# Loads split in place, a second buffer for the folded sequences, and a weight product in the butterfly stage of a post-LN decoder layer

## The chip, the cores and the metric

The kernel runs on one core of a Trainium2 chip. The time is device time in microseconds (us) from the start of the launch to its end. A core has a matrix engine (TensorE; PE in the profile, its weight loads PEld), three engines for elementwise work (VectorE or DVE, ScalarE or ACT, GpSimd or POOL), and SyncE (SP), which here only starts transfers. The on-chip memory has 128 partitions; a tile is partitions x elements. TensorE's results go to a memory of their own (PSUM), in which this kernel's products are 128 x 512 tiles.

## What is computed

A decoder layer on x of shape (4, 1024, 512) in float32, with a context of shape (4, 2048, 384): windowed self-attention, then a cross-attention block, then a feed-forward block whose hidden layer passes two butterfly transforms. What the change touches is this part of the reference:

```python
V = x_vision @ Wv                                   # (., 2048, 384) @ (384, 512)
c_t = einsum('btg,bgd->btd', attn_mean, V)
x = layernorm(x_text, g_norm_in, b_norm_in)
scale_in, shift_in = split(c_t @ W_film_in + b_film_in, 2)    # W_film: (512, 1024)
x = x * (1 + mod_gate * scale_in) + mod_gate * shift_in
Kf = rfft(K, n=2 * L); xf = rfft(x, n=2 * L, axis=1)
y = irfft(xf * Kf.T[None], n=2 * L, axis=1)[:, :L] + x * D_skip
scale_out, shift_out = split(c_t @ W_film_out + b_film_out, 2)
...
h = butterfly(x @ W_exp + b_exp, up_weights)        # 11 stages of 2x2 blocks on 2048 columns
h = butterfly(gelu(h + up_bias), down_weights)
y = h @ W_con + b_con + down_bias
```

## The kernel before

`decoder_layer` (L2985) runs nine stages one behind another: `taps` (L86), `butterfly` (L481), attention, keys, cross-attention, `film` (L1720, the conditioning), `dft` (L2023, the spectrum), `idft` (L2228, the inverse) and the feed-forward parts. A stage allocates its own on-chip tiles, ends at a barrier, and then GpSimd clears its semaphores one by one (L66). Within a stage the order on each engine is written out by hand, with semaphores between engines. A product in full float32 precision is `mm3` (L78): each operand is split into a high half (rounded to fp32r, by a ScalarE copy) and a low half (the difference, by a VectorE subtraction), and three products are added.

**Butterfly.** The stage multiplies the butterflies into the weights beforehand. Each matrix (`wc` = W_con for the down weights, `wT` = W_exp turned for the up weights) takes its four outer butterfly levels as passes over 8 block pairs of 128 rows. For each pair ScalarE scales two partners (`partners`, L647 and L648); for each group of two pairs VectorE makes four sums (`group`, L729 and L734). Four slots of partners lie between them, so ScalarE is at most two groups ahead. The seven inner levels are multiplied out by VectorE into 16 blocks (`low_blocks`, `e_up` and `e_dn`); TensorE multiplies these into `wT` (L597) and, after turning them (L605), into `wc` (L614). The order is: passes 0 to 3 of the first matrix (`wc`), with the copies of the turned W_exp in pass 1 (L673) and of the 16 products in passes 2 and 3; then passes 0 to 3 of the second (`wT`), in whose passes 1 and 2 ScalarE copies the turned down blocks (L655) and the 16 down products; then SyncE stores these (`w4`), and the final rows are turned (L624) and stored (`w3`). ScalarE's and VectorE's first work waits for `s_wc` and `s_cols`, all of W_con and all ten small loads of columns and biases on SyncE's queue.

**Conditioning.** TensorE turns Wv (L1836) and makes 12 blocks Wv times W_film (4 quarters `f` by 3 row blocks `c`, L1848), each of four 128x512 products. ScalarE writes a block's high half times the gate (L1891), VectorE its low half. `wfilm` holds one film matrix, so W_film_out is loaded when six blocks are done. TensorE waits for all 12, then 32 tiles follow, with 4 x 3 x 3 = 36 products each.

**Spectrum.** Four DFT matrices of 128x2048 are loaded by SyncE into the two halves of `raw` in turn, and split (L2144, L2172). Then the taps are loaded into `raw`, TensorE reverses the second half of the rows (L2106), VectorE folds (sum and difference, L2179 and L2180, into `uvf`), and both are split into `uv` (L2150, L2186). Five sequences, taps first and then four of the batch, each have 8 chunks of 24 products. For the taps VectorE makes `kc` and `ks` (L2197 to L2202) from each chunk, for the others four products with them (L2218); GpSimd adds these (L2092, L2093) and ScalarE's queue stores. The fold of the next sequence stands ahead of chunk 6, but `uv` is single: its high halves wait for the last product of the sequence before (L2149), and `split` is the first thing of the next one.

**Inverse.** Four matrices go through the two halves of `mraw`, then eight spectrum chunks through the two of `raw`. The products wait for all four matrices and then for each chunk. Each sequence has four row tiles; TensorE ends one with 8 x 2 x 3 products, and ScalarE copies one half of the result (L2355). The next sequence's chunks are split after the last products that read the old ones (`s_used`), two at a time as `raw` allows.

## Time and profile before

| | us |
|---|---|
| median of 3 runs | 4975.23 (4973.64 to 4977.94) |
| profiled execution | 4974.19 |
| its span, first to last instruction | 4972.5 |
| butterfly stage, from its first transfer | 272.84 |
| conditioning stage | 2468.49 |
| spectrum stage | 2835.96 |
| inverse stage | 3161.19 |

| engine | busy us | share of the span |
|---|---|---|
| TensorE (PE) | 4046.5 | 81% |
| VectorE (DVE) | 2692.0 | 54% |
| ScalarE (ACT) | 1435.4 | 29% |
| GpSimd (POOL) | 1301.9 | 26% |

TensorE is busy for most of the span, but the shares are means over nine stages with different limits. A stage's cost is what stands between its first transfer and the barrier behind it, so the four edited stages are read by their timelines: one line is a run of like instructions of an engine, with its start, its busy time, and in brackets how long the engine had been idle and what released it. In windows each engine has its busy time and count, then come the granted clock as a share of TensorE's full speed (1.00 is 2.4 GHz, 0.50 is 1.2 GHz), the mean share of the transfer engines and the traffic.

### The profile page before, as it was taken

The page shows a single profiled execution, that of the slowest core. Times are in us where ns is not written, and L with a number is a line of the kernel's source. Part 1 is how long each engine was busy: PE and PEld are TensorE (multiplying, and loading weights), DVE is VectorE, ACT ScalarE, POOL GpSimd, SP SyncE. Part 2 cuts the span into 40 slices and gives each one's busy share as a digit, 9 for nine tenths or more (in the row PEclk, how much of TensorE's full clock was granted, in tenths as well). Part 3 has the DMA queues.
Part 4 walks back from the last instruction along what each step waited for, and adds up shares of the span by engine and source line. Part 5 has one row for each costly group of instructions (what it writes and reads, how often), then busy time and mean ns, then how long its engine had stood idle before and what let it go on. Part 6 is the DMA issues. An engine that isn't in the chain of part 4 may idle for free. (4 is left out here: it accounts for less than half of the span.)

```text
span 4972.5 us, 63780 instructions
## 1 busy us (share of the span) xinstructions
PE 4046.5 (81%) x20652; PEld 3295.3 (66%) x20652; DVE 2692.0 (54%) x9090; ACT 1435.4 (29%) x2190; POOL 1301.9 (26%) x1123
## 2 busy tenths in 40 slices
PE   6833898756878866678689788695999999999998
PEld 4712777636767765667658666574888787887886
DVE  8644545438988989989535445322443445322222
ACT  2344333235555544455310000121211112111111
POOL 0000000002121120121136414102576775433332
PEclk8666999878888887788899889897999999999999
DMA  1134222260110100100124422334122223100000
GB/s 56 37 117 119 68 83 79 66 193 28 30 42 12 44 26 10 39 30 12 41 92 140 140 73 110 120 127 139 50 71 65 74 74 99 33 26 20 22 25 20
DMA packets 244966, 329.93 MB, mean 66 GB/s; under 512 B 67013, under 2 KB 125253, under 8 KB 242375
## 3 DMA queue, kind: packets, MB, share of 16 engines
q1 hardware_dynamic: 152568, 175.70, 11.9%
q10 hardware_dynamic: 89568, 142.64, 8.5%
q0 software_dynamic: 2560, 8.39, 0.4%
q8 instruction: 121, 1.98, 0.2%
q14 instruction: 149, 1.21, 0.1%
HBM read 217.55 MB, written 109.10 MB: 66 GB/s over the span
## 5 line engine op out<-in xcount | busy, mean ns | idle before, releaser
L1496 PE MATMUL xa_ps_t<-xa_diag,xa_s_buf 128*128 128x128 f32 x4096 | 503.0, 283 | 161.7 <-DVE xa_s_buf L1677 96.8
L1496 PEld LDWEIGHTS xa_ps_t<-xa_diag,xa_s_buf 128*128 128x128 f32 x4096 | 486.9, 198 | 192.0 <-DVE xa_s_buf L1677 114.3
L1625 DVE MAX8 xa_cand<-xa_s_buf 128x8 f32<-128x64 f32 x4096 | 534.9, 217 | 115.6 <-issue 56.9
L2938 DVE CAST m_act_hl<-m_g 128x512 fp32r<-128x512 f32 x256 | 137.7, 538 | 831.9 <-ACT m_g L2806 831.9
L2632 POOL TENSOR_TENSOR m_act_hl<-m_g,m_act_hl 128x512 fp32r<-128x512 f32 x256 | 355.5, 1389 | 660.0 <-DVE m_act_hl L2938 660.0
L2806 ACT ACTIVATE m_g<-m_ps_h,m_b 128x512 f32<-128x512 f32 x256 | 176.1, 688 | 1096.2 <-PE m_ps_h L82 1091.1
L1441 POOL TENSOR_TENSOR xa_aT<-xa_a,xa_aT 128x512 fp32r<-128x512 f32 x128 | 159.7, 1269 | 1006.6 <-ACT xa_a L1561 1006.6
L80 PE MATMUL m_ps_h<-m_hT,m_w 128*128 128x512 f32 x1024 | 413.7, 404 | 6.4 <-issue 4.3
L80 PE MATMUL m_ps_o<-m_w,m_act_hl 128*128 128x512 f32 x1024 | 406.9, 397 | 0.7 <-POOL m_act_hl L2632 0.7
L82 PE MATMUL m_ps_o<-m_w,m_act_hl 128*128 128x512 f32 x1024 | 406.6, 397 | 0.0
L81 PE MATMUL m_ps_o<-m_w,m_act_hl 128*128 128x512 f32 x1024 | 406.5, 397 | 0.0
L82 PE MATMUL m_ps_h<-m_hT,m_w 128*128 128x512 f32 x1024 | 406.2, 397 | 0.0
L81 PE MATMUL m_ps_h<-m_hT,m_w 128*128 128x512 f32 x1024 | 406.0, 396 | 0.0
L1540 ACT ACTIVATE xa_s_buf<-xa_ps_s 128x2048 f32<-128x2048 f32 x128 | 239.7, 1873 | 403.1 <-PE xa_ps_s L1477 328.6
L1677 DVE SCALAR_TENSOR_TENSOR xa_s_buf<-xa_s_buf,xa_top,xa_prob 128x2048 f32<-128x2048 f32 x128 | 294.7, 2344 | 4.4 <-ACT xa_prob L1551 0.8
L1477 PE MATMUL xa_ps_s<-xa_ks,xa_qs 128*128 128x512 f32 x512 | 189.0, 501 | 105.7 <-ACT xa_s_buf L1540 83.9
L1551 ACT ACTIVATE xa_prob<-xa_s_buf,xa_nmax 128x2048 f32<-128x2048 f32 x128 | 252.4, 2000 | 31.7 <-DVE xa_s_buf L1677 31.7
L80 PE MATMUL xa_ps_ac<-xa_ctx_hl,xa_aT 128*128 128x384 f32 x512 | 206.5, 403 | 50.9 <-POOL xa_aT L1441 50.9
L80 PEld LDWEIGHTS m_ps_h<-m_hT,m_w 128*128 128x128 f32 x1024 | 193.4, 189 | 56.1 <-issue 11.4
L80 PEld LDWEIGHTS m_ps_o<-m_w,m_act_hl 128*128 128x128 f32 x1024 | 193.1, 189 | 48.8 <-POOL m_act_hl L2632 2.0
L82 PEld LDWEIGHTS m_ps_o<-m_w,m_act_hl 128*128 128x128 f32 x1024 | 193.6, 189 | 47.0
L81 PEld LDWEIGHTS m_ps_o<-m_w,m_act_hl 128*128 128x128 f32 x1024 | 193.4, 189 | 47.1
(366 smaller groups left out, 8119.5 us busy)
## 6 DMA issues: line engine op xcount, KB each, us to landing
at_xk<-in_x_dram SPq DMA_DIRECT2D x128, 128.0 KB, 2.7
spectrum<-df_yo ACTq DMA_DIRECT2D x32, 512.0 KB, 2.8
id_raw<-spectrum SPq DMA_DIRECT2D x32, 512.0 KB, 3.8
m_xt<-x ACTq DMA_DIRECT2D x64, 256.0 KB, 3.5
ky_raw<-in_ctx_dram SPq DMA_DIRECT2D x16, 768.0 KB, 6.3
xa_ks<-kt SPq DMA_DIRECT2D x48, 256.0 KB
...
```

The costliest lines, as they stand in the source:

```text
L80: pe.matmul(out, w_hi, m_lo, start=start, stop=False)
L81: pe.matmul(out, w_lo, m_hi, start=False, stop=False)
L82: return pe.matmul(out, w_hi, m_hi, start=False, stop=stop)
L1441: pool.tensor_tensor(aT[:, 1, 4 * g:4 * g + 4, :], a32[:, g % 2, :, :], aT[:, 0, 4 * g:4 * g + 4, :].bitcast(F32), ALU.subtract).then_inc( ...
L1477: last = pe.matmul(ps_s[:, c, :], qs[:, t % 2, h, :], ks[:, h, c * 512:(c + 1) * 512], start=True, stop=True)
L1496: last = pe.matmul(ps_t[:, c // 4, c % 4, :], s_buf[:, t % 2, h, k0:k0 + P], diag[:, h, :], start=(h == 0 and c % 4 == 0), stop=(h == HEAD ...
L1540: act.activation(s_buf[:, t % 2, h, :], ps_s[:, :, :].rearrange("p c n -> p (c n)"), ACT.Copy).then_inc(s_sc, 1)
L1551: act.activation(prob[:, h % 2, :], s_buf[:, t % 2, h, :], ACT.Exp, bias=nmax[:, t % 2, h:h + 1], scale=SCALE).then_inc(s_exp, 1)
L1625: dve.max(out=ranks[h][:, :, g], in_=s_buf[:, t % 2, h, g * SEG:(g + 1) * SEG])
L1677: dve.scalar_tensor_tensor(out=s_buf[:, t % 2, h, :], in0=s_buf[:, t % 2, h, :], scalar=top[:, t % 2, h, TOPK - 1:TOPK], in1=prob[:, h % 2 ...
L2632: pool.tensor_tensor(lo, g32[:, :], hi.bitcast(F32), ALU.subtract).then_inc(s_gl, 1)
L2806: act.activation(g32[:, :], ps_h[:, n % 2, :], ACT.Gelu, bias=b1[:, cur, n:n + 1]).then_inc(s_g, 1)
```

## The change

The diff has four parts, here by stage and with what falls away mostly left out, as it stands in the code above.

**Butterfly.** The order of the loads is new: the down columns first, W_con in four pairs of pieces with a semaphore each, then b_exp, the up columns and the rest; ScalarE starts its loads behind its first pair. The stage also makes the 12 blocks Wv times W_film. Each film matrix is loaded into the memory of `low_up` or `low_dn` once the inner levels of that matrix are multiplied out. TensorE makes six blocks behind the 16 up products, two behind down product 7 and four behind down product 15; VectorE copies the turned Wv between groups of pass 1, and the blocks (times the gate, into `fo`, two slots) between groups of passes 0, 1 and 3 of the second matrix; SyncE stores them to `wf` in DRAM, six ahead of the down rows and six behind.

```diff
+        for k in range(TOP):
+            sp.dma_start(col_dn[:, k, :, :], A["L0_ffn_down_weights"][LOW + k].rearrange("(q p) i j -> p q (i j)", p=P)).then_inc(s_cdn, 16)
...
+            for h in (2 * k, HC // 2 + 2 * k):
+                sp.dma_start(wc[:, h:h + 2, :], A["L0_ffn_W_con"][h * P:(h + 2) * P, :].rearrange("(c p) n -> p c n", p=P))\
+                  .then_inc(s_wc[k], 16)
...
+        for k in range(TOP):
+            sp.dma_start(col_up[:, k, :, :], A["L0_ffn_up_weights"][LOW + k].rearrange("(q p) i j -> p q (i j)", p=P)).then_inc(s_cup, 16)
+        sp.dma_start(low_dn[:, 0:LEN], A["butterfly_down"]).then_inc(s_ld, 16)
...
+        sp.wait_ge(s_wx[1], 16)
+        sp.dma_start(wv[:, :, :], A["L0_xattn_Wv"].rearrange("(c p) n -> p c n", p=P)).then_inc(s_wv, 16)
...
+        for k, (done, name) in enumerate(((s_eu, "in"), (s_ed, "out"))):
+            sp.wait_ge(done, 1)
+            sp.dma_start(films[k], A[f"L0_xattn_W_film_{name}"].rearrange("(c p) n -> p c n", p=P)).then_inc(s_film[k], 16)
+        def film_stored(n):
+            sp.wait_ge(s_fc, n + 1)
+            sp.dma_start(wf_out[n % VC, :, n // VC, :], fo[:, n % 2, :]).then_inc(s_fs[n % 2], 16)
+        for n in range(FILM):
+            film_stored(n)
         for n in range(HC):
             sp.wait_ge(s_dc, n + 1)
             sp.dma_start(w4_out[n * P:(n + 1) * P, :], out_t[:, n % 4, :]).then_inc(s_out[n % 4], 16)
+        for n in range(FILM, 2 * FILM):
+            film_stored(n)
...
+        def film(n):
+            k, q, c = n // FILM, n % FILM // VC, n % VC
+            if n % FILM == 0:
+                pe.wait_ge(s_film[k], 16)
+                pe.wait_ge(s_wvc, VC)
+            if n >= 2:
+                pe.wait_ge(s_fc, n - 1)
+            for e in range(DC):
+                last = pe.matmul(ps_w[:, n % 2, :], wvT[:, e, c * P:(c + 1) * P], films[k][:, e, q * D:(q + 1) * D],
+                                 start=(e == 0), stop=(e == DC - 1))
+            last.then_inc(s_fp, 1)
...
-        pe.wait_ge(s_cols, 16 * 10)
+        pe.wait_ge(s_cup, 16 * 5)
         pe.wait_ge(s_eu, 1)
...
+        for n in range(FILM):
+            film(n)
...
+            if h == HC // 2 - 1:
+                film(FILM)
+                film(FILM + 1)
+        for n in range(FILM + 2, 2 * FILM):
+            film(n)
...
+        act.wait_ge(s_cdn, 16 * 4)
         for q in range(HC // 2):
+            if q % 2 == 0:
+                act.wait_ge(s_wc[q // 2], 32)
             partners(0, 0, q)
+            if q == 0:
+                act.dma_start(low_up[:, 0:LEN], A["butterfly_up"]).then_inc(s_lu, 16)
+                w_exp(0)
+                w_exp(1)
+        act.wait_ge(s_cup, 16 * 5)
...
+        def film_copied(n):
+            dve.wait_ge(s_fp, n + 1)
+            if n >= 2:
+                dve.wait_ge(s_fs[n % 2], 16 * (n // 2))
+            dve.tensor_scalar(fo[:, n % 2, :], ps_w[:, n % 2, :], gate[:, 0:1], None, ALU.mult).then_inc(s_fc, 1)
+        dve.wait_ge(s_cdn, 16 * 4)
         for g in range(GROUPS):
+            dve.wait_ge(s_wc[g], 32)
             group(0, 0, g)
...
+                if i == 1 and g < VC:
+                    dve.wait_ge(s_wvt, g + 1)
+                    dve.tensor_copy(wvT[:, :, g * P:(g + 1) * P], ps_w[:, g % 2, :].rearrange("p (e q) -> p e q", e=DC))\
+                       .then_inc(s_wvc, 1)
...
+                if i == 0:
+                    film_copied(g)
+                if i == 1 and GROUPS + g < FILM:
+                    film_copied(GROUPS + g)
+                if i == TOP - 1:
+                    film_copied(FILM + g)
+        for n in range(FILM + GROUPS, 2 * FILM):
+            film_copied(n)
```

```diff
+    wf = scratch("wf", [VC, P, 4, D])
+    stage_butterfly(nc, A, w3, b3, w4, wf)
...
+    stage_film(nc, A, wf, x1, ac, xin, so, sh)
```

**Conditioning.** The products are gone. Four chunks of 768 KB come from `wf` into `raw`, which is the memory of the low half of the tile `wf`; ScalarE writes the high halves, VectorE the low ones in place, and the first tile's products wait for one chunk at a time.

```diff
+wf = sb("wf", [P, 2, NF, VC, D], F32R)
+raw = nc.alloc_sbuf_tensor_at("fi_raw", [P, NF, VC, D], F32, offset=at + 4 * NF * VC * D)
...
+            sp.dma_start(raw[:, f, :, :], wf_in[:, :, f, :].rearrange("c p n -> p c n")).then_inc(s_wf[f], 16)
...
+                if first:
+                    pe.wait_ge(s_fol, f + 1)
+                else:
                     pe.wait_ge(s_fr, NF * (t - 1) + f + 1)
...
+        def weights_hi(f):
+            act.wait_ge(s_wf[f], 16)
+            act.activation(wf[:, 0, f, :, :], raw[:, f, :, :], ACT.Copy).then_inc(s_foh, 1)
...
+        def weights_lo(f):
+            dve.wait_ge(s_foh, f + 1)
+            dve.tensor_tensor(wf[:, 1, f, :, :], raw[:, f, :, :], wf[:, 0, f, :, :].bitcast(F32), ALU.subtract).then_inc(s_fol, 1)
...
+        dve.wait_ge(s_ld, 16 * 5)
+        dve.tensor_scalar(bf[:, :, :], bf[:, :, :], gate[:, 0:1], None, ALU.mult)
...
         norm(0, 0)
+        for f in range(NF):
+            weights_lo(f)
+        dve.drain()
         tiles(dve, tile)
```

**Spectrum.** All four matrices are loaded at once, each into the memory of its own low half (`mraw`), two by SyncE behind the taps and two by ScalarE. The fold is done in place in `x`. `uv` has two buffers. The high halves of a sequence wait for the sequence before the last; for the batch the fold stands ahead of chunk 5 and the split ahead of chunk 7, for the first of them (`split(1)`) behind the taps' last chunk. The loops are written out.

```diff
+mraw = nc.alloc_sbuf_tensor_at("df_mraw", [P, 2, 2, TC, 512], F32, offset=at + 4 * 2 * 2 * TC * 512)
...
+x = sb("x", [P, 2, TC, D])
+uv = sb("uv", [P, 2, 2, 2, TC, D], F32R)
...
+        def load(src, first, n):
+            if n:
+                sp.wait_ge(s_lo, 2 * n)
...
+            sp.dma_start(x[:, 0, :, :], rows(src, first, S // 2).rearrange("(q p) d -> p q d", p=P)).then_inc(s_x, 16)
+        load(taps, 0, 0)
+        for n in (1, 3):
+            sp.dma_start(mraw[:, n // 2, n % 2, :, :], A["dft"][n // 2, n % 2].rearrange("(q p) m -> p q m", p=P)).then_inc(s_m[n], 16)
+        for b in range(B):
+            load(xin, b * S, b + 1)
...
                 if q == 0:
                     pe.wait_ge(s_lo, 2 * n + 1 + src)
+                if n == 0 and mq == 0:
+                    pe.wait_ge(s_ml, 2 * par + sd + 1)
...
+        for n in (0, 2):
+            act.dma_start(mraw[:, n // 2, n % 2, :, :], A["dft"][n // 2, n % 2].rearrange("(q p) m -> p q m", p=P)).then_inc(s_m[n], 16)
+        act.dma_start(tw[:, :, :], A["twiddle"].rearrange("i (q p) -> p i q", p=P), allow_slow_non_contiguous=True).then_inc(s_tw, 16)
...
         def hi(n):
             act.wait_ge(s_uv, n + 1)
-            act.wait_ge(s_f, MC * n)
+            if n >= 2:
+                act.wait_ge(s_f, MC * (n - 1))
             for i in range(2):
-                act.activation(uv[:, i, 0, :, :], uvf[:, i, :, :], ACT.Copy).then_inc(s_hi, 1)
...
+        matrix_hi(0)
+        hi(0)
+        for n in range(1, 4):
+            matrix_hi(n)
+        hi(1)
...
+                if q == MC - 2 and b + 2 <= B:
...
+            dve.tensor_tensor(x[:, 1, :, :], x[:, 0, :, :], ps_rev[:, :, :], ALU.subtract)
+            dve.drain()
+            dve.tensor_tensor(x[:, 0, :, :], x[:, 0, :, :], ps_rev[:, :, :], ALU.add)
...
         fold(0)
+        matrix_lo(0)
         split(0)
+        for n in range(1, 4):
+            matrix_lo(n)
...
+            if q == MC - 1:
+                split(1)
+        for b in range(B):
             for q in range(MC):
-                k = q % 2
...
+                if q == MC - 3 and b + 2 <= B:
                     fold(b + 2)
...
+                if q == MC - 1 and b + 2 <= B:
+                    split(b + 2)
```

**Inverse.** All matrices and all chunks are loaded at once, in place as well; a chunk has its own place and semaphore, and is reloaded when its last product of the sequence before is done.

```diff
+y = sb("y", [P, 2, MC, 2, D], F32R)
+mraw = nc.alloc_sbuf_tensor_at("id_mraw", [P, 2, 2, TC, 512], F32, offset=at + 4 * 2 * 2 * TC * 512)
+raw = nc.alloc_sbuf_tensor_at("id_raw", [P, MC, 2, D], F32, offset=at + 4 * 2 * 2 * 2 * TC * 512 + 4 * MC * 2 * D)
...
+        def chunk(b, q):
+            if b:
+                sp.wait_ge(s_used, MC * (b - 1) + q + 1)
+            sp.dma_start(raw[:, q, :, :], y_in[b:b + 1, q].rearrange("o i p d -> p (o i) d")).then_inc(s_y[q], 16)
...
+        chunk(0, 0)
+        matrix(1)
+        chunk(0, 1)
+        matrix(3)
+        for q in range(2, MC):
+            chunk(0, q)
+        for b in range(1, B):
             for q in range(MC):
...
+                chunk(b, q)
...
+                        if first and t == 0 and mq == 0:
+                            pe.wait_ge(s_ml, 2 * par + pm + 1)
...
+        for n in (0, 2):
...
-        hi(0)
+        hi(0, 0)
+        for n in range(2):
+            matrix_hi(n)
+        for q in range(1, 4):
+            hi(0, q)
+        for n in range(2, 4):
+            matrix_hi(n)
+        for q in range(4, MC):
+            hi(0, q)
```

Two engines' rows show what stands where. First TensorE in the butterfly stage, from the last up products to the turning of the down blocks (`bf_e_dn`), before:

```order
L596 MATMUL bf_ps_b<-bf_wT,bf_e_up 128x1 [waits bf_block_product_copied]
L597 MATMUL bf_ps<-bf_wT,bf_e_up 128x512
L605 MATMUL bf_ps_e<-bf_ident,bf_e_dn 128x128 [waits bf_groups_done,bf_down_blocks,bf_block_product_copied]
L605 MATMUL bf_ps_e<-bf_ident,bf_e_dn 128x128
L614 MATMUL bf_ps<-bf_wc,bf_eT 128x512 [waits bf_down_matrix_transposed_copied]
L605 MATMUL bf_ps_e<-bf_ident,bf_e_dn 128x128 [waits bf_down_matrix_transposed_copied]
```

and now (the left-out rows are three more blocks like the last shown; L666 was L605 and L675 was L614):

```order
L656 MATMUL bf_ps<-bf_wT,bf_e_up 128x512
L644 MATMUL bf_ps_w<-bf_low_up,bf_wvT 128x512 [waits bf_value_weights_turned_copied,bf_film_loaded0]
L644 MATMUL bf_ps_w<-bf_low_up,bf_wvT 128x512 x7
L644 MATMUL bf_ps_w<-bf_low_up,bf_wvT 128x512 [waits bf_film_product_copied]
L644 MATMUL bf_ps_w<-bf_low_up,bf_wvT 128x512 x3
...
L666 MATMUL bf_ps_e<-bf_ident,bf_e_dn 128x128 [waits bf_groups_done,bf_down_blocks,bf_block_product_copied]
L666 MATMUL bf_ps_e<-bf_ident,bf_e_dn 128x128
L675 MATMUL bf_ps<-bf_wc,bf_eT 128x512 [waits bf_down_matrix_transposed_copied]
```

Six blocks have moved between the up products and the down blocks; those from the third on wait for VectorE's copy.

VectorE in the spectrum stage at a change of sequence: the products of the last chunk and what follows, before:

```order
L2218 TENSOR_TENSOR df_prod<-df_ps,df_kc 128x512
L2218 TENSOR_TENSOR df_prod<-df_ps,df_ks 128x512
L2218 TENSOR_TENSOR df_prod<-df_ps,df_kc 128x512
L2218 TENSOR_TENSOR df_prod<-df_ps,df_ks 128x512
L2222 REGISTER_ALU
L2222 COMPARE_AND_BRANCH
L2186 TENSOR_TENSOR df_uv<-df_uvf,df_uv 128x2048 x2
L2218 TENSOR_TENSOR df_prod<-df_ps,df_kc 128x512
```

and now, from the fold ahead of chunk 5 (the L2269 rows are the products that were L2218, four to a chunk):

```order
L2226 TENSOR_TENSOR df_x<-df_x,df_ps_rev 128x2048
L2228 TENSOR_TENSOR df_x<-df_x,df_ps_rev 128x2048
L2269 TENSOR_TENSOR df_prod<-df_ps,df_kc 128x512
L2269 TENSOR_TENSOR df_prod<-df_ps,df_ks 128x512
L2269 TENSOR_TENSOR df_prod<-df_ps,df_kc 128x512
L2269 TENSOR_TENSOR df_prod<-df_ps,df_ks 128x512
L2269 TENSOR_TENSOR df_prod<-df_ps,df_kc 128x512
L2269 TENSOR_TENSOR df_prod<-df_ps,df_ks 128x512
L2269 TENSOR_TENSOR df_prod<-df_ps,df_kc 128x512
L2269 TENSOR_TENSOR df_prod<-df_ps,df_ks 128x512
L2234 TENSOR_TENSOR df_uv<-df_x,df_uv 128x2048 x2
L2269 TENSOR_TENSOR df_prod<-df_ps,df_kc 128x512
```

The two splits have moved from behind the sequence's last chunk to ahead of it, and the fold to two chunks ahead of them.

## Rows read from the trace of the kernel before

**Rows 1.** Timeline of the conditioning stage's start (columns as its first line), then windows, TensorE

```profile
start us, us, engine line op out<-in xcount [idle before <-releaser]
2468.49 0.34 SPq L1789 DMA_DIRECT2D fi_gate<-in_L_xattn_mod_gate_dram  x1
2483.85 1.28 DVE L1938 TENSOR_SCALAR fi_bf<-fi_bf,fi_gate 128x2048 f32<-128x2048 f32 x1 [48.97 <-DMA fi_bf<-_L_xattn_b_film_out_dram]
2485.22 0.76 DVE L1941 TENSOR_SCALAR fi_bf<-fi_bf 128x512 f32<-128x512 f32 x2
2487.54 22.95 PE L1848 MATMUL fi_ps_w<-fi_wfilm,fi_wvT 128*128 128x512 f32 x48 [0.69 <-ACT fi_wvT L1885]
2518.46 22.85 PE L1848 MATMUL fi_ps_w<-fi_wfilm,fi_wvT 128*128 128x512 f32 x48 [7.97 <-DMA fi_wfilm<-_L_xattn_W_film_out_dram]
2548.35 0.80 PE L80 MATMUL fi_ps_f<-fi_wf,fi_aT 128*128 128x512 f32 x1
...
core 0: us, PE busy (x), PEclk, DMA share, GB/s
2487.50:2493.30 5.80, 5.76 (x9) 0.63 0.00 0
2552.50:2560.00 7.50, 7.50 (x34) 0.95 0.01 3
```

**Rows 2.** Timeline of the spectrum stage from its start to its first product

```profile
2835.96 0.38 SPq L2066 DMA_DIRECT2D df_tw<-in_twiddle_dram  x1
2844.91 2.29 DVE L2172 TENSOR_TENSOR df_mats<-df_raw,df_mats 128x2048 fp32r<-128x2048 f32 x1 [14.70 <-ACT df_mats L2144]
2867.94 1.19 PE L2106 MATMUL df_ps_rev<-df_raw,df_flip 128*128 128x512 f32 x1 [38.52 <-DMA df_raw<-taps]
2883.59 0.79 PE L80 MATMUL df_ps<-df_uv,df_mats 128*128 128x512 f32 x1 [8.94 <-DVE df_uv L2186]
```

**Rows 3.** Timeline of spectrum stage at two changes of sequence, and a chunk's window

```profile
2932.84 0.75 DVE L2197 TENSOR_SCALAR df_prod<-df_ps,df_tw 128x512 f32<-128x512 f32 x1 [0.26 <-PE df_ps L82]
2946.11 0.69 DVE L2218 TENSOR_TENSOR df_prod<-df_ps,df_kc 128x512 f32<-128x512 f32 x1 [5.56 <-PE df_ps L82]
2990.91 2.89 DVE L2186 TENSOR_TENSOR df_uv<-df_uvf,df_uv 128x2048 fp32r<-128x2048 f32 x1 [0.73 <-issue]
2991.61 3.33 POOL L2093 TENSOR_TENSOR df_yo<-df_prod 128x512 f32<-128x512 f32 x1
...
core 0: us, PE busy (x) PEld busy (x) DVE busy (x) ACT busy (x) POOL busy (x), PEclk, DMA share, GB/s
...
3118.56:3124.00 5.44, 5.44 (x25) 4.50 (x24) 2.48 (x4) 0.00 (x0) 2.53 (x2) 1.00 0.26 96
```

**Rows 4.** Timeline of the inverse stage: first product, and row tiles' ends on ScalarE

```profile
3184.29 0.77 PE L80 MATMUL id_ps<-id_y,id_mats 128*128 128x512 f32 x1 [33.12 <-DVE id_y L2373]
3206.56 0.60 ACT L2355 ACTIVATE id_a_sb<-id_ps 128x512 f32<-128x512 f32 x1 [3.02 <-PEq L2320]
3229.92 0.60 ACT L2355 ACTIVATE id_a_sb<-id_ps 128x512 f32<-128x512 f32 x1 [10.33 <-PEq L2320]
3257.60 0.60 ACT L2355 ACTIVATE id_a_sb<-id_ps 128x512 f32<-128x512 f32 x1 [2.16 <-PEq L2320]
3269.78 0.60 ACT L2355 ACTIVATE id_a_sb<-id_ps 128x512 f32<-128x512 f32 x1 [10.24 <-PEq L2320]
```

**Rows 5.** Timeline of the butterfly stage's start: first transfer, ScalarE's first work

```profile
272.84 0.39 SPq L550 DMA_DIRECT2D bf_wc<-in_L_ffn_W_con_dram  x1
310.47 0.72 ACT L647 ACTIVATE bf_part<-bf_wc,bf_col_dn 128x512 f32<-128x512 f32 x1 [41.48 <-DMA bf_upb<-in_L_ffn_up_bias_dram]
321.66 0.58 ACT L673 ACTIVATE bf_wT<-bf_ps 128x512 f32<-128x512 f32 x1
```

**Rows 6.** Windows of the butterfly stage (columns as in Rows 3), and one timeline row

```profile
316.22:319.25 3.03, 0.00 (x0) 0.00 (x0) 2.83 (x5) 2.56 (x5) 0.00 (x0) 0.50 0.00 0
411.22:413.08 1.86, 1.22 (x4) 0.44 (x3) 1.03 (x3) 1.86 (x6) 0.00 (x0) 1.00 0.41 149
...
392.97 1.22 PE L614 MATMUL bf_ps<-bf_wc,bf_eT 128*128 128x512 f32 x1 [12.83 <-ACT bf_eT L655]
```

**Rows 7.** Windows of transfers: both queues (Rows 3's columns), then SyncE's alone

```profile
281.00:289.00 8.00, 1.91 (x8) 1.51 (x8) 0.00 (x0) 0.00 (x0) 0.00 (x0) 0.50 1.00 418
...
core 0: us, , PEclk, DMA share, GB/s
2863.00:2864.00 1.00, 0.50 1.04 406
```

314 lines of the change are left out of this document (119 added, 195 removed).

## Prediction

> **What bounds the kernel now.** The stages stand one behind another, each ended by a barrier, so each is read by itself. I read the timeline by engine from a stage's first transfer to its first product, then the places where TensorE stops in the steady part, and the windows for clock and traffic. Outside four stages nothing is edited.
>
> The conditioning stage has its first transfer at 2468.49 and its first tile product at 2548.35: 79.9 us in which TensorE makes 12 folded blocks, six behind each 2 MB load [rows 1]. A block is 48/6 = 8 records, 3.43 us at full clock; VectorE's share of it never waits on anything but this product. The stage behind that is TensorE's.
>
> The spectrum stage goes from 2835.96 to 2883.59 (47.6 us) without a product [rows 2]: four matrices through two buffers, then the taps, then reverse, fold and split in a row. Afterwards TensorE runs a chunk in 5.44 us (distance of two of VectorE's product groups, 3118.56 to 3124.00) and stops at each change of sequence: 2932.84 to 2946.11 is 13.27 instead of 5.44 [rows 3].
>
> The inverse stage starts its products at 3184.29, 23.1 us in; its first row tile ends 22.3 us later, where a later one takes 12.2 (3257.60 to 3269.78); a change of sequence makes two tiles last 27.7, 28.1 and 28.3 (the first is in [rows 4]) instead of 24.4.
>
> The butterfly stage is bound by ScalarE and VectorE in turns. Nothing is computed from 272.84 to 310.47, since ScalarE waits for the last of eleven loads [rows 5]. Then VectorE needs 3.03 us per group of block pairs (316.22 to 319.25), and in the two middle passes of the second matrix ScalarE needs 1.86 per pair (411.22 to 413.08) [rows 6].
>
> **Transfers.** One queue alone moves 406 GB/s, two queues together 418 [rows 7]. So I divide all bytes on both queues by 400 GB/s and let two queues share evenly. The Trainium skill (DMA: Bandwidth & Descriptors, section "Issuing engines are not separate DMA queues") says that starting transfers from two engines saves only the issue. The rows agree; were the queues additive instead, the taps would land 5 us earlier.
>
> **Conditioning stage: minus 56.4.** Transposes, 24 + 24 products and the 12 evictions go. Left ahead of the first tile are the loads. They ended at 2483.85 with 4.25 MB on one queue; now it is 5.4 MB with the tile loads, 1.15 MB or 2.9 us more: 2486.7. Then the bias scaling (1.28 + 2 x 0.76 with its drains, 2.9), the normalisation of 512 columns (0.57) and the low half of the first block, 1536 columns (1.72), both at 2.29 us per 2048 [rows 2]: product at 2491.9. 2548.35 - 2491.9 = 56.4; the other three low halves (5.2) lie beside the first tile's 10.7 us of products. Bounds: loads at 2484 or 2490, 53 to 59.
>
> **Spectrum stage, start: minus 18.** Six MB go at once. The taps (2 MB, SyncE's queue) come in while ScalarE's queue moves two matrices: 4 MB, 10.5 us, behind 1.9 of start and with 1.2 to the reversal as before: 2849.5 instead of 2867.94. The chain from there took 15.65 us; it gets 0.4 longer, as the first matrix's low half (2.29) now stands between fold and split and only 1.9 of it lies beside ScalarE's copy. If the taps' queue is served first, 23; if served last, 13.
>
> **Spectrum stage, changes of sequence: minus 19.** The excess over 5.44 is 7.8 (2932.84 to 2946.11), 8.2, 9.5 and 8.6, by the same reading. The second buffer lets ScalarE's and VectorE's split run ahead, but the split of the first sequence is written behind VectorE's last tap chunk, so it starts at the time it has now: no gain there. For the other three, VectorE folds before chunk 5 and splits before chunk 7. ScalarE's copies end 5.4 us after chunk 6's products, VectorE's first half then lands 0.4 us past the end of chunk 7, and its last products 1.1 past. That is 1.1 us with nothing in the way. Against it stands that the split now meets GpSimd's sums: where they met, VectorE's half took 2.89 instead of 2.29 and GpSimd's op 3.33 instead of 1.3 [rows 3]. That adds up to 2. I take 2.3 each: 26.3 - 6.9 = 19 (16 to 23).
>
> **Inverse stage: minus 21.5.** 8 MB start at once. By the same rate matrix 0 lands at 3169.5, its halves are done at 3173.8, and the product starts some 10.5 us earlier. Matrix 3 is complete at 3187.6 and the eight chunks' low halves follow every 1.2 us to 3192.5, so the first tile ends near 3195.5 instead of 3206.56: 11 (7 if TensorE is at its low level there). At a change of sequence a chunk is reloaded when its last product is done: 1.3 us of transfer, 3.6 to land, 2.3 to split, needed 12.2 after. It fits with 4 us to spare, so 3.3 + 3.7 + 3.9 = 10.9 goes; I take 10.5.
>
> **Butterfly stage: plus 11.** Here work is added to the engines that bound it.
> 1. The columns come first and the big weight in four parts, so pass one starts near 281.5 and ends near 297, 28 us earlier. But ScalarE's copies of the turned up-weight wait for the up-columns, which stand behind the 4 MB and share with ScalarE's own 4 MB: about 301 instead of 321.66 [rows 5]. Lead 20.7.
> 2. VectorE copies the turned value weights between its groups of pass two, and TensorE turns these behind all 16 up-weight groups. VectorE waits, and ScalarE's next pairs wait for VectorE: the lead falls to 15.
> 3. In the second matrix's first pass stand four gated copies (about 0.7 us each, by L2197's 0.75 in [rows 3]). TensorE makes blocks 2 to 5 in it, each waiting for the copy two before; the last ends near 388. Only then does it turn the down blocks, and ScalarE waits for those (TensorE waits 12.8 us for its copy ahead of 392.97 now [rows 6]; it would be 380): lead 4.
> 4. SyncE stores block 5 ahead of the first down rows, so ScalarE's fifth eviction finds its buffer unstored: 4.2. Lead 0.
> 5. Blocks 6 and 7 stand between down products 7 and 8: 6.9 us less 2 of slack: lead -5.
> 6. Blocks 8 to 11 are tied to the last pass's groups; the last ends 6 us behind VectorE's last group, and the final transposes wait for it: lead -11.
> So the stage ends 11 us later. Bounds: -3 (loads 4 us earlier, half of 3 to 5 absent) to +25 (the blocks at TensorE's low level, 6.9 instead of 3.43 us, as the 0.63 clock at 2487.5 shows for the first [rows 1]). Fourteen more semaphores to clear, ten in the other stages: 1 us.
>
> **Sum.** 56.4 + 18 + 19 + 21.5 - 11 - 1 = 102.9. The profiled execution took 4974.19 us, 1.04 under the median: 4871.
>
> **Rivals.**
> - *The fold really hides.* If steps 3 to 5 cost nothing, the stage ends 15 - 6 = 9 us earlier instead of 11 later: 4851, and 4845 with the taps served first. For it: TensorE is idle for 12.8 us ahead of 392.97. Against: each wait named above stands ahead of the next in its engine's own order.
> - *Low clock for the blocks.* They come in spells with idle time between: +14 at half of them, 4885; +27 at all, 4898.
> - *VectorE and GpSimd block each other.* Both halves and both sums of a change alternate, and the split ends as late as now: up to 19 back, 4890. The Trainium skill (SBUF - State Buffer, section "SBUF: two separate sides") has a VectorE op with two SBUF inputs and a GpSimd op exclude each other for a whole instruction. By that rule GpSimd's 1.3 plus the rest of a 2.25 half is 3.3, which the trace agrees with.
> - *Slower than before.* TensorE enters the conditioning tiles without 46 us of products ahead. If it then stayed at its low level in them, a tile's 36 products would take 15.4 instead of 8.4 us: 7 us per tile, 32 tiles, 5095. It turns slower from the 15th such tile on. Against it: from 2552.5 the clock is 0.95 after 4 us of unbroken products [rows 1].
> - *Not what it says:* the first change of sequence, counted above.
>
> **How the numbers follow.** Forecast 0.66 (4858 to 4884), hidden fold 0.12, low clock 0.11, mutual blocking 0.09, slower 0.02. The range 4846 to 4896 leaves out the slow case, half of the hidden fold's tail and the full low clock. 0.2% is 10 us, about what a measurement can tell; all cases but the last lie over 70 us below: faster 0.97, same 0.01, slower 0.02.
>
> **What would show it.** First tile product 23 to 24 us behind the conditioning stage's first transfer; first spectrum product 29 to 30 us in; three of four changes of sequence under 3.5 us of excess, the first still near 8; inverse changes near zero; in the butterfly stage first work about 9 us in, SyncE's first down-row store late, and a stage end some 11 us later. I am wrong if products at a stage's start wait for another load, or if the butterfly's end comes earlier.

## Result and the profile after

The changed kernel takes 4882.44 us (median of 4 runs, 4880.04 to 4883.11) against 4975.86 (4973.64 to 4977.94): 0.9813 of the time before, with a 95% interval of 0.9801 to 0.9825. The forecast was 4871 with a range of 4846 to 4896: the direction and the range hold, and 11 us of the gain are missing.

The profiled execution took 4882.0 us with a span of 4880.3, against 4972.5 of span before. The page's first lines, engines (busy us, share of the span):

```profile
span 4880.3 us, 63397 instructions
...
PE 4037.1 (83%) x20652; PEld 3291.2 (67%) x20652; DVE 2698.5 (55%) x9097; ACT 1431.6 (29%) x2179; POOL 1299.0 (27%) x1123
```

TensorE does as many products as before (20652). Its busy time has fallen by 9.4 us (4046.5 to 4037.1); the rest of the gain, 82.8 us, is idle time. Where it went is read from the stages' starts. GpSimd clears a tile at the start of each stage, in the timeline (start, busy us, engine, line, tile, idle before and its releaser):

```profile
272.54 0.20 POOL L608 MEMSET bf_ident<- 128x128 f32 x1 [11.07 <-POOLq L66]
485.70 0.20 POOL L985 MEMSET at_ident<- 128x128 f32 x1 [212.46 <-POOLq L66]
2489.03 0.20 POOL L1884 MEMSET fi_ident<- 128x128 f32 x1 [15.39 <-POOLq L66]
2798.04 0.20 POOL L2073 MEMSET df_flip<- 128x128 f32 x1 [7.15 <-POOLq L66]
3091.68 0.20 POOL L2073 MEMSET id_flip<- 128x128 f32 x1 [4.96 <-POOLq L66]
3321.61 0.20 POOL L2653 MEMSET m_ident<- 128x128 f32 x1 [6.94 <-POOLq L66]
```

Differences of neighbouring starts give the stages; of the kernel before they come from the same rows of its trace.

| stage | before, us | after, us | difference | forecast |
|---|---|---|---|---|
| butterfly | 196.6 | 213.2 | +16.6 | +11 |
| conditioning | 367.5 | 309.0 | -58.5 | -56.4 |
| spectrum | 325.2 | 293.6 | -31.6 | -37 |
| inverse | 249.9 | 229.9 | -20.0 | -21.5 |
| all that is not edited | 3833.3 | 3834.6 | +1.3 | 0 |
| clearing of the new semaphores | | in the stages | | +1 |

The +1.3 of the last row but one is mostly spread. Over all twelve profiled kernels, this one and the one before among them, the cross-attention took 1400.5 to 1407.2 us and the attention 511.3 to 514.6. The stage of the keys is less clear: 84.5 us in the kernel before and 86.1 to 88.1 in all eleven others. With one profile of the kernel before, the runs don't show whether the change has a part in that. Each run also repeats stages whose code is the same as in another: in five profiles the changed butterfly stage took 211.5 to 213.2 us. So a difference of under 2 us between two stages says little.

**Conditioning.** The biases' load ends the wait 18.2 us into the stage, and the first tile product comes 22.6 us in (79.9 before, at 2548.35 in [rows 1]). Timeline, then windows (us, PE busy and count, granted clock, DMA share, GB/s):

```profile
2507.26 1.29 DVE L2040 TENSOR_SCALAR fi_bf<-fi_bf,fi_gate 128x2048 f32<-128x2048 f32 x1 [7.88 <-DMA fi_bf<-_L_xattn_b_film_out_dram]
2511.66 0.77 PE L80 MATMUL fi_ps_f<-fi_wf,fi_aT 128*128 128x512 f32 x1 [10.92 <-DVE fi_wf L1998]
...
2511.00:2513.00 2.00, 1.34 (x3) 0.50 0.00 0
2513.00:2515.00 2.00, 2.00 (x6) 0.50 0.00 0
2515.00:2520.00 5.00, 5.00 (x22) 0.97 0.00 0
```

The granted clock is 0.50, the lower level of 1.2 GHz, until 2515 and 0.97 behind it, after 3.3 us of unbroken products. So the tiles don't stay at the low level for want of the fold ahead of them.

**Spectrum.** The reversal starts 13.9 us in and the first product 28.9 us in [rows 2: 32.0 and 47.6]. Then a change of sequence as before (the taps' last chunk to the first of the next sequence), and a later one, from chunk 6's products over the split to the next sequence's first:

```profile
2811.94 1.19 PE L2155 MATMUL df_ps_rev<-df_x,df_flip 128*128 128x512 f32 x1 [20.45 <-DMA df_x<-taps]
2826.91 0.80 PE L80 MATMUL df_ps<-df_uv,df_mats 128*128 128x512 f32 x1 [9.44 <-DVE df_uv L2234]
...
2876.96 0.75 DVE L2248 TENSOR_SCALAR df_prod<-df_ps,df_tw 128x512 f32<-128x512 f32 x1
2890.47 0.69 DVE L2269 TENSOR_TENSOR df_prod<-df_ps,df_kc 128x512 f32<-128x512 f32 x1 [6.00 <-PE df_ps L82]
...
2926.58 0.69 DVE L2269 TENSOR_TENSOR df_prod<-df_ps,df_kc 128x512 f32<-128x512 f32 x1 [0.78 <-PE df_ps L82]
2931.05 2.92 DVE L2234 TENSOR_TENSOR df_uv<-df_x,df_uv 128x2048 fp32r<-128x2048 f32 x1 [1.99 <-ACT df_uv L2198]
2941.50 0.69 DVE L2269 TENSOR_TENSOR df_prod<-df_ps,df_kc 128x512 f32<-128x512 f32 x1 [2.93 <-PE df_ps L82]
```

The first change takes 13.51 for one chunk, 8.07 over the 5.44 of [rows 3]. The later one takes 14.92 for two chunks, 4.04 over 10.88; the other two read the same way give 4.02 and 3.98. VectorE waits 1.99 us for ScalarE's half ahead of the split. That was not in my sum.

**Inverse.** First product 12.8 us in, first row tile's end 35.4 us in [rows 4: 23.1 and 45.4]; the two tiles at a change take 24.4 (3150.43 to 3174.81), twice a single one:

```profile
3104.46 0.76 PE L80 MATMUL id_ps<-id_y,id_mats 128*128 128x512 f32 x1 [22.93 <-DVE id_mats L2432]
3127.06 0.60 ACT L2412 ACTIVATE id_a_sb<-id_ps 128x512 f32<-128x512 f32 x1 [7.35 <-PEq L2377]
3150.43 0.60 ACT L2412 ACTIVATE id_a_sb<-id_ps 128x512 f32<-128x512 f32 x1 [10.33 <-PEq L2377]
3174.81 0.60 ACT L2412 ACTIVATE id_a_sb<-id_ps 128x512 f32<-128x512 f32 x1 [4.14 <-PEq L2377]
```

**Butterfly.** Rows of the timeline of ScalarE, VectorE and SyncE, in order of time:

```profile
281.06 0.72 ACT L713 ACTIVATE bf_part<-bf_wc,bf_col_dn 128x512 f32<-128x512 f32 x1 [12.35 <-DMA bf_wc<-in_L_ffn_W_con_dram]
322.64 0.69 DVE L825 COPY bf_wvT<-bf_ps_w 128x512 f32<-128x512 f32 x1 [8.65 <-PE bf_ps_w L632]
390.06 0.28 ACT L721 ACTIVATE bf_eT<-bf_ps_e 128x128 f32<-128x128 f32 x1 [8.82 <-PE bf_ps_e L666]
...
401.21 0.32 SPq L588 DMA_DIRECT2D wf<-bf_fo  x1
401.58 0.43 SPq L594 DMA_DIRECT2D w<-bf_out_t  x1
404.12 0.60 ACT L727 ACTIVATE bf_out_t<-bf_ps 128x512 f32<-128x512 f32 x1 [4.96 <-DMA w<-bf_out_t]
416.19 0.28 ACT L721 ACTIVATE bf_eT<-bf_ps_e 128x128 f32<-128x128 f32 x1 [5.85 <-PE bf_ps_e L666]
...
451.09 0.75 DVE L811 TENSOR_SCALAR bf_fo<-bf_ps_w,bf_gate 128x512 f32<-128x512 f32 x1 [2.25 <-PE bf_ps_w L644]
454.52 0.75 DVE L811 TENSOR_SCALAR bf_fo<-bf_ps_w,bf_gate 128x512 f32<-128x512 f32 x1 [2.68 <-PE bf_ps_w L644]
```

ScalarE starts 8.5 us in instead of 37.6 [rows 5], and then five waits follow: VectorE 8.65 us for TensorE to turn Wv, ScalarE 8.82 for the down blocks turned behind block 5, 4.96 for a down row's store that stands behind block 5's on SyncE's queue, 5.85 behind blocks 6 and 7, and at the end VectorE for the last two blocks. These two are 3.43 us apart: a block at full clock. Not all blocks ran so. TensorE's rows, then windows (us, PE busy and count, granted clock, DMA share, GB/s):

```profile
373.32 16.59 PE L644 MATMUL bf_ps_w<-bf_low_up,bf_wvT 128*128 128x512 f32 x32 [10.60 <-DVE bf_fo L811]
437.62 16.87 PE L644 MATMUL bf_ps_w<-bf_low_dn,bf_wvT 128*128 128x512 f32 x32 [8.72 <-DVE bf_fo L811]
...
373.30:379.60 6.30, 6.28 (x9) 0.58 0.23 88
437.60:444.20 6.60, 6.58 (x9) 0.56 0.21 79
444.20:454.50 10.30, 10.30 (x26) 1.00 0.20 76
```

These are blocks 2 to 5 and blocks 8 to 11. TensorE had been idle for 10.60 and 8.72 us ahead of them, and the first block of each run took 6.3 and 6.6 us at a granted clock of 0.58 and 0.56. Four blocks at full clock are 13.7 us, so the two runs are 2.9 and 3.2 us longer. The first ends where the down blocks are turned, for which ScalarE waits 8.82; the second ends in VectorE's last copy.

### The profile page after: what moved, and what is told of

It is laid out like the page before. It is cut to its first block and busy times, and to the rows that moved or that the text cites. A ratio compares the mean times of both kernels' runs of the same rounds, so it can differ in the third digit from the quotient of the medians.

```text
span 4880.3 us, 63397 instructions
## 1 busy us (share of the span) xinstructions
PE 4037.1 (83%) x20652; PEld 3291.2 (67%) x20652; DVE 2698.5 (55%) x9097; ACT 1431.6 (29%) x2179; POOL 1299.0 (27%) x1123
## 3 DMA queue, kind: packets, MB, share of 16 engines
q1 hardware_dynamic: 151976, 177.79, 12.2%
## 5 line engine op out<-in xcount | busy, mean ns | idle before, releaser
L80 PE MATMUL xa_ps_ac<-xa_ctx_hl,xa_aT 128*128 128x384 f32 x512 | 206.7, 404 | 48.1 <-POOL xa_aT L1530 48.1
L80 PEld LDWEIGHTS m_ps_h<-m_hT,m_w 128*128 128x128 f32 x1024 | 193.3, 189 | 55.9 <-issue 11.3
L80 PEld LDWEIGHTS m_ps_o<-m_w,m_act_hl 128*128 128x128 f32 x1024 | 193.2, 189 | 48.6 <-POOL m_act_hl L2705 2.0
L82 PEld LDWEIGHTS m_ps_o<-m_w,m_act_hl 128*128 128x128 f32 x1024 | 193.5, 189 | 46.9
L82 PEld LDWEIGHTS m_ps_h<-m_hT,m_w 128*128 128x128 f32 x1024 | 193.5, 189 | 46.9
```

The lines of the kernel that those rows point to most:

```text
L80: pe.matmul(out, w_hi, m_lo, start=start, stop=False)
L82: return pe.matmul(out, w_hi, m_hi, start=False, stop=stop)
```

## Experiments

Of the kernels below all but the last two were run once; they are compared by the stages of their profiles. The lead used below is worked out from VectorE's timeline: the start of its n-th group of block pairs, counted from the stage's start, in the kernel before less that in the kernel at hand.

### The new order of loads alone

The kernel before with only this part of the diff, no block in the stage:

```diff
-sp.dma_start(wc[:, :, :], A["L0_ffn_W_con"]...).then_inc(s_wc, 16)
+for k in range(TOP):
+    sp.dma_start(col_dn[:, k, :, :], ...).then_inc(s_cdn, 16)
+for k in range(4):
+    for h in (2 * k, HC // 2 + 2 * k):
+        sp.dma_start(wc[:, h:h + 2, :], ...).then_inc(s_wc[k], 16)
```

> The kernel before with the new order of loads of the butterfly stage alone: no products of Wv and W_film in it, the conditioning, spectrum and inverse stages as before. In the changed kernel VectorE's groups stand 20.0 us earlier in the stage at the end of pass one than before, and the stage ends 16.6 us later. If the new order of loads is worth that lead and everything given back comes from the 12 blocks, the stage takes 196.6 - 18 = about 178 us (some 2 us less than the 20, as W_exp's first rows are asked for 8 us later), and the run about 4957 us. Rival: the lead cannot be kept in any case, because the copies of the turned W_exp in pass 1 wait for rows of W_exp that are asked for later and share the engines with W_con; then the stage takes 188 to 197 us and the run 4967 to 4975.

Measured: stage 177.4 us, run 4958.6. The lead is 28.9 us at the first group, 20.9 at the end of pass 0 (ScalarE waits 4.8 us each for W_con's third and fourth pair of pieces, which are under way together with W_exp), and 19.2 to 19.4 from the second group of pass 2 to the last. So this order is worth 19.2 us for good, and the 12 blocks, their loads, copies and stores cost 213.2 - 177.4 = 35.8 us where they stand.

### One store moved

```diff
-for n in range(FILM):
+for n in range(4):
     film_stored(n)
 for n in range(HC):
+    if n in (2, 4):
+        film_stored(3 + n // 2)
     sp.wait_ge(s_dc, n + 1)
```

> The changed kernel with one thing moved: SyncE stores blocks 4 and 5 behind down rows 1 and 3 instead of ahead of down row 0. In the changed kernel ScalarE waits 4.96 us for a down row's store in the middle of the second matrix's pass 1. If this wait is on the path, as my step 4 has it, the butterfly stage takes 213.2 - 5 = 208 us and the run 4877. Rival: ScalarE's wait only covers one that is there anyway, the next one (for the down blocks turned behind blocks 6 and 7) grows by what is saved, and the stage stays within 1 us of 213.

Measured: stage 206.7 us, 6.5 less; run 4879.63. The wait was on the path. The table below shows it between groups 21 and 22. The 1.5 us beyond the 4.96 are within what the same stage varies by.

### The blocks spread over the stage

The pieces on TensorE; copies and stores follow them.

```diff
     pe.matmul(ps[:, h % 2, :], blk, wT[:, h, 0:D], start=True, stop=True).then_inc(s_mm, 1)
-for n in range(FILM):
-    film(n)
+    if h >= HC // 2:
+        film_part((h - HC // 2) // DC, h % DC)
+film(2)
...
 down_turned(0)
+down_turned(1)
+film(3)
+film(4)
+film(5)
...
-    if h == HC // 2 - 1:
-        film(FILM)
-        film(FILM + 1)
-for n in range(FILM + 2, 2 * FILM):
+    film_part(FILM + h // DC, h % DC)
+for n in range(FILM + 4, 2 * FILM):
     film(n)
```

> The changed kernel with the 12 blocks at other places of the butterfly stage, the same instructions otherwise: the turned Wv copied in pass 2 instead of 1 of the first matrix; blocks 0 and 1 one product at a time behind up products 8 to 15, block 2 behind those; both first down blocks turned ahead of blocks 3 to 5; blocks 6 to 9 one product at a time behind the 16 down products; only blocks 10 and 11 behind them; copies and stores to match. If the cost of the blocks is that others wait for TensorE in order, and not their work, the lead of some 20 us is mostly kept: stage 213 - 28 = 185 us (180 to 192), run about 4854. Rival: TensorE itself is the bound in the second matrix (its low clock makes a block 6.9 us), then the stage takes over 200 us.

Measured: stage 191.9 us, 21.3 less than in the changed kernel; run 4861.07. The blocks now cost 14.5 us. I expected 185, so 7 us of the gain are missing, but the rival's 200 did not come. The products are the same in both; it is who waits behind them that changed. The rest of the loss was read from this trace. VectorE waits for the store of block 0, which SyncE holds behind the load of W_film_out, and ScalarE for VectorE in turn:

```profile
372.55 0.75 DVE L825 TENSOR_SCALAR bf_fo<-bf_ps_w,bf_gate 128x512 f32<-128x512 f32 x1 [3.35 <-DMA wf<-bf_fo]
376.25 0.72 ACT L727 ACTIVATE bf_part<-bf_wT,bf_col_up 128x513 f32<-128x513 f32 x1 [4.36 <-DVEq L819]
```

### ScalarE's copies

```diff
+def film_scaled(n):
+    act.wait_ge(s_fp, n + 1)
+    act.wait_ge(s_fs[n % 2], 16 * (n // 2))
+    act.wait_ge(s_fc, n)
+    act.activation(fo[:, n % 2, :], ps_w[:, n % 2, :], ACT.Copy, scale=gate[:, 0:1]).then_inc(s_fc, 1)
...
         partners(1, i, q)
+        if i == 0 and q % 2:
+            film_scaled(2 + q // 2)
+        if i == TOP - 1 and q in (1, 4, 7):
+            film_scaled(FILM + 3 + q // 3)
...
+sp.wait_ge(s_wx[1], 32)
 for k, (done, name) in enumerate(((s_eu, "in"), (s_ed, "out"))):
...
+    if k == 0:
+        film_stored(0)
```

> The kernel with the blocks spread over the butterfly stage (191.9 us), with the waits that its trace shows taken away: the store of block 0 ahead of the load of W_film_out on SyncE (VectorE waited 3.35 us for it), W_film_in loaded behind the last rows of W_exp (2.3 us lost in pass 1), the stores of blocks 6 to 8 behind two more down rows (1.33 and 1.18 us), and the copies in the passes that VectorE bounds (0 and 3, seven of 0.7 us) made by ScalarE. If each of these is on the path by itself, the stage takes 191.9 - 3.4 - 2.3 - 2.5 - 4.9 = 179 us, within 2 us of the stage without any block (177.4). Rival: ScalarE at 2.46 of 3.03 us per group has no room for a copy of 0.6 and its waits, and the stage stays over 185 us.

Measured: stage 185.9 us, run 4856.47. I expected 179. The copies in passes 0 and 3 are free on ScalarE (the lead stays at 11.2 to 11.6 through pass 3, where VectorE's copies took 0.7 each); the wait for block 0's store is gone, but another of the same length stands in its place, ahead of the copy of block 3. ScalarE's row, SyncE's two, the time from the second of these to its landing, and a window of TensorE:

```profile
372.16 0.69 ACT L749 ACTIVATE bf_fo<-bf_ps_w,bf_gate 128x512 f32<-128x512 f32 x1 [3.35 <-issue]
...
362.26 0.37 SPq L589 DMA_DIRECT2D bf_low_dn<-_L_xattn_W_film_out_dram  x1
363.10 0.34 SPq L584 DMA_DIRECT2D wf<-bf_fo  x1
...
DMA to landing us min/median/max: 9.0/9.0/9.0
...
362.90:369.20 6.30, 6.17 (x10) 0.61 0.91 282
```

The timeline calls the releaser "issue", that is, it shows none. In its order ScalarE waits there for block 3 and for the store of block 1, whose slot the copy takes. Block 3's eight products (with two turned down blocks the ten of the window) had ended by 369.2, at a granted clock of 0.61. The store of block 1 started at 363.10, just behind the 2 MB load of W_film_out, and took 9.0 us to land, where a store of a block takes 2.3 in the median: 372.1. So it is again a store behind that load on SyncE, now block 1's, and the lead falls from 16.7 to 13.2.

The lead in us, by group (0 to 15 are the first matrix, 16 to 31 the second, four to a pass):

| group | loads alone | changed kernel | store moved | spread | ScalarE's copies |
|---|---|---|---|---|---|
| 3, end of pass 0 | 20.9 | 20.0 | 18.4 | 19.4 | 19.7 |
| 5, after the first copy of Wv | 20.9 | 10.9 | 9.6 | 19.4 | 19.7 |
| 15, end of the first matrix | 19.4 | 12.6 | 11.1 | 16.6 | 17.3 |
| 19, end of the second's pass 0 | 19.3 | 10.5 | 9.0 | 10.7 | 13.3 |
| 20, pass 1 starts | 19.2 | 3.2 | 2.8 | 10.3 | 12.5 |
| 22, in pass 1 | 19.3 | -1.8 | 2.9 | 10.5 | 11.7 |
| 24, pass 2 starts | 19.2 | -7.8 | -1.9 | 8.9 | 11.6 |
| 31, last group | 19.2 | -10.1 | -4.1 | 5.3 | 11.3 |

### The conditioning stage's order on VectorE

```diff
+for f in range(NF):
+    weights_lo(f)
 dve.wait_ge(s_ld, 16 * 5)
 dve.tensor_scalar(bf[:, :, :], bf[:, :, :], gate[:, 0:1], None, ALU.mult)
...
 norm(0, 0)
-for f in range(NF):
-    weights_lo(f)
```

> The changed kernel with VectorE's low halves of the four weight chunks ahead of the scaling of the biases in the conditioning stage. In the changed kernel VectorE waits until 18.2 us into the stage for the bias vectors, which are loaded last, though the first weight chunk's high half is done 10 us in; the first tile product comes at 22.6 us. If that order is what holds the first product, it comes 11 to 12 us in and the stage takes 309.0 - 9 = 300 us; the run 4873. Rival: the first tiles are then bound by the weight chunks' arrival and by GpSimd and VectorE at the biases, which the first results need as well, so that less than 3 us is gained.

Measured: first product 12.2 us into the stage, stage 299.9 us, 9.1 less; run 4871.87.

```profile
2496.70 3.42 DVE L1998 TENSOR_TENSOR fi_wf<-fi_raw,fi_wf 128x1536 fp32r<-128x1536 f32 x2
2498.59 0.77 PE L80 MATMUL fi_ps_f<-fi_wf,fi_aT 128*128 128x512 f32 x1 [0.20 <-DVE fi_wf L1998]
```

So the changed kernel waited for the vectors that are loaded last with data in hand that came first.

### The spectrum stage's changes of sequence

Three kernels: ScalarE's high halves one chunk earlier; the taps' fold and split where those of the others stand; both, with the two halves of the split parted.

```diff
-if q == MC - 2 and b + 2 <= B:        # ScalarE
+if q == MC - 3 and b + 2 <= B:
     hi(b + 2)
```

> The changed kernel with one thing moved: ScalarE's high halves of the next sequence of the batch stand behind its store of chunk 4 instead of chunk 5 in the spectrum stage. In the changed kernel the three later changes of sequence cost 4.0 us each, not the 2.3 of my sum, and VectorE waits 1.99 us for ScalarE's half ahead of the split. If ScalarE's late start is the cause, the split begins when chunk 6's products are done and each change costs 4.0 - 1.9 = 2.1 us: spectrum stage 293.7 - 5.6 = 288 us. Rival: VectorE and GpSimd block each other and the split ends as late as now (4.0 us each, stage 293 to 294).

```diff
-    if q == MC - 2:
+    if q == MC - 3:
         fold(1)
+    if q == MC - 1:
+        split(1)
...
-    if q == MC - 1:
-        split(1)
```

> The changed kernel with the taps' fold ahead of chunk 5 and their split of the first sequence ahead of chunk 7, as for the others, instead of behind chunk 7. In the changed kernel the first change of sequence costs 8.07 us. If only the place of the split makes it so, it costs some 2 us (ScalarE's halves are early there, and GpSimd has nothing to do yet): stage 293.7 - 6 = 288 us. Rival: the taps' chunks take VectorE 3.0 us with its drains and are twice as dependent, and the fold ahead of chunk 5 delays TensorE in chunk 6 or 7; then under 3 us is gained.

```diff
-        if q == MC - 1 and b + 2 <= B:
-            split(b + 2)
+        if q >= MC - 2 and b + 2 <= B:
+            split(b + 2, (q - MC + 2,))
```

> The changed kernel with both of these moves and the two halves of a split parted: one ahead of chunk 6's products and one ahead of chunk 7's. If the time of a change is only what VectorE has queued behind the last chunk's end, each of the four costs 1 us or less: 20.1 us of them become 3, stage 293.7 - 17 = 277 us, run 4866. Rival: GpSimd's sums and VectorE's halves now meet twice at each change and stretch each other, so that a change costs 3 us and the stage takes 285.

Measured: stages 286.6, 284.3 and 277.1 us (293.6 in the changed kernel); runs 4878.42, 4879.15 and 4870.84. With ScalarE's halves early a later change costs 1.64 us instead of 4.04 (12.52 for two chunks, first and last row); the others read the same way 1.67 and 1.65. VectorE's half and GpSimd's sums meet there:

```profile
2927.17 0.69 DVE L2269 TENSOR_TENSOR df_prod<-df_ps,df_kc 128x512 f32<-128x512 f32 x1 [0.78 <-PE df_ps L82]
2929.86 1.29 POOL L2144 TENSOR_TENSOR df_yo<-df_prod 128x512 f32<-128x512 f32 x1 [0.71 <-DVEq L2271]
2929.87 3.42 DVE L2234 TENSOR_TENSOR df_uv<-df_x,df_uv 128x2048 fp32r<-128x2048 f32 x1 [0.22 <-issue]
2931.10 3.34 POOL L2145 TENSOR_TENSOR df_yo<-df_prod 128x512 f32<-128x512 f32 x1
2939.69 0.69 DVE L2269 TENSOR_TENSOR df_prod<-df_ps,df_kc 128x512 f32<-128x512 f32 x1 [0.71 <-PE df_ps L82]
```

The half takes 3.42 instead of 2.29 [rows 2] and the sum 3.34 instead of 1.3. In this kernel and in the one with parted halves the halves of the later changes take 3.1 to 3.4; in the changed kernel, where ScalarE's lateness held the split back by 1.99 us, the first half took 2.92, the second 2.28, and no sum was longer than 1.3. So here the meeting is the price of the earlier start: two halves take 6.7 us instead of 4.6, and 1.6 us of the change remain. What the change would cost without the meeting was not run. Moving the taps' split took the first change from 8.07 to 0.31 us over two chunks (11.19 from the taps' chunk 6, 2873.41 to 2884.60). Parted halves give 1.14 to 1.19 for a later change, taken over four chunks, 0.5 less than whole ones. The 20.1 us of the four changes become 3.8 by these readings, and the stage fell by 16.5.

### All together

The butterfly stage with ScalarE's copies, the parted split and the conditioning stage's order; then the same with the copies of blocks 3 to 5 later:

```diff
-        if i == 0 and q % 2:
-            film_scaled(2 + q // 2)
+        if i == 0 and q in (1, 4, 6):
+            film_scaled(2 + q // 3)
...
-        if i == 1 and g == 2:
-            film_copied(FILM)
+        if i == 1 and g in (0, 3):
+            film_copied(5 + g // 3)
```

> The changed kernel with the butterfly stage of the run with ScalarE's copies (185.9 us there), the parted splits in the spectrum stage (277.1 us) and the low halves ahead of the bias scaling in the conditioning stage (299.9 us). If the stages are independent, as the barrier between them has it, the gains add: 4882.4 - 27.3 - 9.1 - 16.5 = 4829.5 us (4826 to 4833), 0.971 of the kernel before. Rival: a stage that ends with TensorE busier or idler changes the clock of the next, so that the sum misses by more than 4 us.

> The same with the copies of blocks 3 to 5 later in the butterfly stage: ScalarE waited 3.35 us for block 3 in pass 0, and VectorE stood behind it. Block 3 is copied behind pair 4 instead of 3, block 4 behind pair 6 instead of 5, block 5 by VectorE behind pass 1's first group; the stores of blocks 5 and 6 stand behind three and two more down rows. If that wait is on the path, 1 to 3 us are saved: stage 183 to 185 us, run 4827 to 4829. Rival: TensorE is the bound there (blocks 2 to 5 in a row are 13.7 us of work), the wait comes back at the first down product, and nothing changes.

Measured, against 4974.45 us of the kernel before on the same chip: 4831.0 us (4829.74 to 4833.49), a ratio of 0.9712 with an interval of 0.9695 to 0.9728; and 4831.64 (4830.52 to 4835.52), 0.9714 with 0.9698 to 0.9730. The gains add within 2 us. The late copies change nothing: butterfly stages of 187.3 and 187.2 us. The outcome is the rival's, but not for its reason. ScalarE's wait ahead of block 3's copy shrank from 3.22 to 1.88 us; it ends at 370.75, and the store of block 1, again behind the load of W_film_out, started at 361.78 and landed 8.9 us later, at 370.7. The lead in pass 1 is 14.8 us instead of 10.0, but in pass 2 it is back at 10.0, for TensorE waited for a copy of VectorE's:

```profile
396.11 1.50 PE L650 MATMUL bf_ps_w<-bf_low_dn,bf_wvT 128*128 128x512 f32 x2 [3.07 <-DVE bf_fo L837]
```

That is the copy of block 6, for which block 8 waits, and which this edit had put behind the last group of pass 1, one group later than before. So the wait was on the path, and what its shortening gave was lost at the next place in the order; that TensorE's work is the bound is not shown. What is left of the blocks' cost, 187.3 - 177.4 = 9.9 us, was not taken apart further.

## Why the prediction was right, and where it missed

**Transfers and starts.** Dividing all bytes by the rate of one queue was right. The reversal was predicted 13.5 us into the spectrum stage and started 13.9 in; the biases of the conditioning stage landed 18.2 us in, as predicted; the first product came 22.6 in against 23.4. This gave the largest term: 58.5 against 56.4, inside its bounds of 53 to 59. The spectrum's first product came 28.9 us in, 18.7 earlier (forecast 18). About 0.9 of it is given back: from the first product to the first chunk's third operation on VectorE (2837.07) it is 10.16 us, against 9.28 before, with the granted clock at its low level for longer (0.50 for the first 5 us; before, 1.00 from 4.4 us on). The inverse stage's first tile ended 10.0 us earlier instead of 11, and its changes of sequence gave 10.7 instead of 10.5.

**Changes of sequence.** The first stayed as it was, 8.07 against 7.83, because its split stands behind the last tap chunk: as forecast. For the others the step that failed is the 2.3 us each. They cost 4.0. ScalarE's halves stand behind the store of chunk 5, and so behind GpSimd's sums of it; my time for them was too early. Moving them took 2.4 of the 4.0 away. The 1.6 that remain come with VectorE and GpSimd meeting, which by itself was not tested. The excesses of the three before were also a little less than I read: 8.0, 9.5 and 8.5, together 26.0 and not 26.3. 13.7 us were gained where I had 19.

**Butterfly.** The waits came one by one as forecast, and nearly all were larger. Steps against measured leads: after pass 0 20.7 against 20.0; after the copies of Wv 15 against 10.9 (12.6 later); at the second matrix's pass 1, 4 against 3.2; behind the store 0 against -1.8; behind blocks 6 and 7, -5 against -7.8; at the end -11 against -17.2 (the bias addition behind the last copy: 182.65 us into the stage against 165.48). The last step is the one that failed by the most: 9.4 us (from -7.8 to -17.2) where it had 6. The gated copies in pass 3 make VectorE's last group 2.3 later and 7.1 follow behind it, but the end is set by TensorE: it starts block 8 behind the copy of block 6 (437.6), makes the four blocks in 16.9 us without a stop, and the last copy follows. I had each block at 3.43; block 8 took 6.6 at a granted clock of 0.56. These 3 us are nearly the whole miss of the step. Block 2 lost 2.9 the same way ahead of the down blocks' turn. By these rows the low clock of two blocks, some 6 us on the path, is as much as the stage missed its forecast by; that is an estimate, since no run took it away by itself. The miss of 4 us at Wv was half recovered later, since ScalarE could run on.

**Rivals.** The hidden fold did not happen: that rival had the stage 9 us earlier, it ended 16.6 later, and by the loads-alone run the blocks cost 35.8 us. Low clock for the blocks came true in part: two of the twelve (2 and 8), some 6 us, where the rival had 14 at half of them. That the tiles of the conditioning stage might stay slow: the clock was 0.97 after 3.3 us. Mutual blocking of VectorE and GpSimd is real, but the changed kernel lost only 0.6 us to it at a change (2.92 instead of 2.29). The Trainium skill (SBUF - State Buffer, section "SBUF: two separate sides") has them exclude each other for a whole instruction. The trace agrees, as the rows of the kernel with ScalarE's halves early show. A sum runs from 2929.86 to 2931.15; the half that starts at 2929.87, just behind it, has those 1.28 us to wait, is 1.1 longer and ends at 2933.29; the sum that starts at 2931.10 ends at 2934.44, 1.2 behind the half. The stretch is uneven only because each had a different rest of the other's to wait for.

**The missing 11 us** are thus, in the profiled executions, 5.6 in the butterfly stage, 5.4 in the spectrum stage, 1.5 in the inverse stage and 1.3 in stages that nobody edited, less 2.1 in the conditioning stage and less the 1 for semaphores, which the stages' times hold: 10.7, of 102.9 forecast against 92.2. That the total came within 0.3% of the forecast is partly luck: the conditioning stage gave 2.1 more than its sum.
